# Three moves around an attention phase: late statistics of two sequences, a table preload one block earlier, bias pieces made after the plan

## The chip, the cores and the metric

The kernel runs on one core of a Trainium2 chip. A core has five engines that run side by side and meet only at semaphores: TensorE (PE in the profile, its weight loads PEld), VectorE (DVE), ScalarE (ACT), GpSimd (POOL) and SyncE (SP, which here only issues DMAs). The metric is the device time in microseconds of one launch; lower is better. All data are fp32 unless said otherwise.

## The reference, cut to what matters

Input x is 16 sequences of 512 tokens with 128 features. Two layers follow, each a mixing part and an expert part around a residual, with a LayerNorm and a per-sequence modulation ahead of each:

```python
h = layernorm(x) * (1 + ca) + sa;  x = x + ga * ssm(h)          # layer 0: gate, 16-state recurrence per feature, LayerNorm
h = layernorm(x) * (1 + cb) + sb;  x = x + gb * moe0(h)         # layer 0: 8 experts, the best one per token
h = layernorm(x) * (1 + ca) + sa;  x = x + ga * linear_attention(h)   # layer 1: 16 heads, softplus of q and k
h = layernorm(x) * (1 + cb) + sb;  x = x + gb * moe1(h)         # layer 1: 8 experts, swiglu, the best two per token
```

`layernorm` needs for each token the mean and the variance over its 128 features. Softplus is computed as relu(z) plus a corrected log(1 + exp(-|z|)). The second matrix of `moe1` has a bias b2 per expert (8 x 128 numbers), which a matmul adds.

## The kernel before, in words

The tokens stay in SBUF in one buffer `x_tok`: partition = token within a tile of 128, then 64 tiles of 128 features; a sequence is C = 4 tiles. B is 16. The program is a chain of blocks with a barrier between them (`end_phase`, L67: all engines meet, the phase's semaphores are cleared, all engines meet again). The blocks that matter:

**The mixture** (layer 0's experts, to L1143). Each engine has its instructions for sequences w = 0 to 15 in an order written out by hand. For each w, DVE masks the features by expert (`mask`), PE multiplies (`product`), ACT scales the result (`scaled`), PE turns it back and DVE adds it to `x_tok` (`added`). Behind that stand the statistics that the next LayerNorm needs: DVE sums a sequence (`sum_x2`), ACT squares it with an accumulating output, four instructions and four reads (`squares_2`), and POOL makes from both the factor `rs2` = (variance + eps)^-0.5 and the shift `shift2` = -mean * rs2 (`mean_2`, `scale_2`). So `rs2` and `shift2` of all 16 sequences are there when the block ends.

**The attention** (from L1389). All engines but SP run a written loop of bodies n; in body n each works on several sequences at once, each at another stage. DVE's body n holds `correction(n)`, `logits(n - 5)`, the softplus of n, four `weighted(n - 1, c)`, `moments(n - 2)` (bn_stats and bn_aggr of the tokens after the attention) and `added(n - 5)`. PE waits in its `states` for the softplus. ACT numbers its bodies three ahead of DVE: ACT's body n holds `exponentials(n - 3)` and also `norm0(n)`, which normalizes sequence n's tokens with `rs2` and `shift2`; it is the only reader of these two. ACT uses Ln and Exp in turn, which one table set holds; at the block's start ACT loads that set (L1721).

At the block's start SP issues small loads one after the other: keys' bias, weights, b2 (into a part of `xg`, the buffer of layer 0 that the attention doesn't use, called `room`), 8 loads of `bv`, 8 of `wo`, last the router's weights and their bias `gb`. DVE's opening instructions split two biases into bf16 pieces whose sum is the fp32 value: the keys' bias (`bkf`, L1812) and b2 (`b2f` into `b2x`, L1819 to L1828), the latter a memset, then twice a cast, a product and a subtraction, then a cast, on 3 partitions of 1024 numbers. Then DVE waits for `gb` (L1829), sets up constants and enters the loop.

POOL multiplies keys and values (`products`, L1515) and sends each token's normalized features to its two experts' rows in DRAM (`send`, L1524: 128 indirect DMAs, eight per sequence, in the kernel's text scatters).

**The plan** (from L2066). When the last sequence's experts are known, DVE works out how many tiles each expert has and where each starts, in a chain of short instructions that ends with `packs` (L2107); its widest use two scratch tensors `ge` and `gst` in `room`. SP waits for all scatters and for the plan, then loads the first rows.

**The experts of layer 1** (to the end): 72 tiles of 256 rows. PE multiplies (L2494, L2515) and adds b2 from `b2x` (L2510), from its third tile on; DVE and ACT work on both halves of the product.

## Time and profile before

| what | value |
|---|---|
| time, median of 3 runs | 981.67 us (980.34 to 982.22) |
| profiled execution | 986.01 us, span 984.10 us |
| PE busy | 839.7 us, 85% of the span |
| DVE busy | 775.3 us, 79% |
| ACT busy | 658.5 us, 67% |
| POOL busy | 562.5 us, 57% |
| chain that ended last | PE 52%, DVE 3%, DMA 3%, issue 2% |

The span runs from the first to the last instruction of the profiled execution; around it lie 1.91 us that belong to its time. An engine's busy share says little by itself, since the phases have different limits; the page's slices show the phases:

```profile
PE   6978891699999939999999999998306999999991
```
```profile
DVE  2988678899998766779999999999753666666996
```
```profile
PEclk9989795699999969999999999999557999999996
```

Each digit is a slice of 24.6 us, in tenths; PEclk is the clock granted to PE, in tenths of full speed. The mixture ends in slice 14, the attention runs to slice 28, the plan lies in slices 28 to 30, and the experts of layer 1 fill the rest.

### The profile page before, as it was taken

Reading aid. Unit: us, or ns where it says so; the run is one execution under the profiler, and the core shown is the slowest. Engines: PE = TensorE matmul, PEld = TensorE weight load, DVE = VectorE, ACT = ScalarE, POOL = GpSimd, SP = SyncE. Lnnn points to the kernel's source line nnn. Section 1 sums busy time; section 2 is a strip of 40 time slices with the busy share of each in tenths; the row PEclk is TensorE's granted clock in tenths of the full one; section 3 lists DMA queues with packets and bytes.
Section 4 is the critical chain, followed back from the end, with each engine's and each line's share of the span. In section 5 each row is a group of like instructions: output and inputs, shape, how many; then the busy total and the mean of one; then the engine's idle time right before and its main releaser. Section 6 shows DMA issues by size and latency. Waiting matters only on the chain.

```text
span 984.1 us, 23471 instructions
## 1 busy us (share of the span) xinstructions
PE 839.7 (85%) x7426; PEld 649.8 (66%) x7441; DVE 775.3 (79%) x2069; ACT 658.5 (67%) x1737; POOL 562.5 (57%) x573
## 2 busy tenths in 40 slices
PE   6978891699999939999999999998306999999991
PEld 5945570354445428888888888887105889889880
DVE  2988678899998766779999999999753666666996
ACT  3557127899995375667777787764605888888880
POOL 1211007747873325343888888888772666666773
PEclk9989795699999969999999999999557999999996
DMA  5330262233233121000111111111125655555977
GB/s 149 91 92 1 87 174 61 97 130 114 98 129 114 60 45 46 2 1 21 37 35 37 35 45 37 34 37 42 47 94 157 221 182 178 183 182 187 338 247 252
DMA packets 83813, 101.31 MB, mean 103 GB/s; under 512 B 15390, under 2 KB 65497, under 8 KB 81516
## 3 DMA queue, kind: packets, MB, share of 16 engines
q1 hardware_dynamic: 71100, 79.46, 25.5%
q0 software_dynamic: 8704, 18.11, 5.3%
q10 hardware_dynamic: 3888, 2.25, 0.7%
q8 instruction: 62, 1.02, 0.4%
q14 instruction: 59, 0.48, 0.2%
HBM read 76.11 MB, written 23.67 MB: 101 GB/s over the span
## 4 chain that ended last, share of the span: by engine, by line
PE 52%; DVE 3%; DMA 3%; issue 2%; POOL 1%; ACT 1%; SPq 1%; ACTq 0%; POOLq 0%; DVEq 0%
PE ps L2494 13%; PE ps L2251 11%; PE ps L2515 6%; PE ps L2267 3%; PE ps L2329 2%; PE ps L2242 2%; PE ps L2477 2%; PE ps L2213 2%; PE ps L2388 2%; PE ps L2368 2%; PE ps L2262 2%; PE ps L2228 1%; POOL rows_of L1524 1%; PE ps L2316 1%; DMA parts<-gx,dest 1%
## 5 line engine op out<-in xcount | busy, mean ns | idle before, releaser
L1524 POOL DMA_INDIRECT rows_of<-payb,posu x128 | 146.1, 1141 | 40.6 <-issue 27.1
L1515 POOL TENSOR_TENSOR kvb<-qk,v 128x1024 f32<-128x1024 f32 x64 | 126.1, 1975 | 75.0 <-DVE qk L1889 50.3
L1115 PE MATMUL ps<-masked,ew 128*128 128x512 f32 x256 | 130.0, 623 | 4.1 <-DVE masked L1043 3.5
L2251 PE MATMUL ps<-con,kvb 128*128 128x128 f32 x1024 | 126.0, 276 | 0.0
L2251 PEld LDWEIGHTS ps<-con,kvb 128*128 128x128 f32 x1024 | 119.4, 192 | 1.0 <-issue 1.0
L2176 DVE TENSOR_SCALAR qk<-ps,b 128x256 f32<-128x256 f32 x144 | 62.9, 478 | 69.7 <-PE ps L2494 67.1
L1549 POOL DMA_INDIRECT parts<-h,dest x72 | 71.0, 986 | 52.5 <-ACT h L1791 38.5
L1043 DVE TENSOR_TENSOR masked<-f_t,wide 128x512 f32<-128x512 f32 x128 | 88.3, 707 | 9.8 <-PE ps L1115 9.5
L1865 DVE TENSOR_TENSOR qc<-ps,qk 128x1024 f32<-128x1024 f32 x64 | 78.1, 1220 | 18.4 <-PE ps L2251 17.8
L1549 POOL DMA_INDIRECT parts<-gx,dest x72 | 73.6, 1023 | 32.6 <-issue 17.4
L2515 PE MATMUL ps<-w,f_t 128*128 x576 | 76.1, 275 | 0.0
L2515 PEld LDWEIGHTS ps<-w,f_t 128*128 128x128 f32 x576 | 70.0, 192 | 8.3
L1115 PEld LDWEIGHTS ps<-masked,ew 128*128 128x128 f32 x256 | 43.4, 194 | 46.9 <-issue 24.0
L1777 ACT ACTIVATE qk<-ps,b 128x256 f32<-128x256 f32 x144 | 60.5, 471 | 17.3 <-PE ps L2494 16.6
L2494 PE MATMUL ps<-qd,ex 128*128 128x256 f32 x288 | 69.5, 385 | 0.0
L2494 PE MATMUL ps<-qd,lg 128*128 128x256 f32 x288 | 68.2, 380 | 0.0
L2494 PEld LDWEIGHTS ps<-qd,ex 128*128 128x128 f32 x288 | 53.0, 194 | 6.0
L1782 ACT ACTIVATE nrm<-qk,limit 128x512 f32<-128x512 f32 x72 | 52.0, 723 | 7.2 <-ACT qk L1777 0.4
L891 ACT ACTIVATE junk<-x_tok,stat 128x128 f32<-128x128 f32 x128 | 49.4, 387 | 10.4 <-DVE stat L1019 9.8
L2142 DVE SCALAR_TENSOR_TENSOR f_t<-qk,nrm 128x512 f32<-128x512 f32 x72 | 49.9, 693 | 7.8 <-ACT nrm L1782 1.0
L2494 PEld LDWEIGHTS ps<-qd,lg 128*128 128x128 f32 x288 | 51.9, 190 | 5.8 <-ACT qd L1762 0.2
L1762 ACT ACTIVATE qd<-ps,ns 128x256 f32<-128x256 f32 x72 | 34.2, 474 | 30.4 <-PE ps L2477 30.4
(347 smaller groups left out, 2133.5 us busy)
## 6 DMA issues: line engine op xcount, KB each, us to landing
wide<-hot_dram SPq DMA_DIRECT2D x16, 1024.0 KB, 4.6
kvb<-rows_of SPq DMA_DIRECT2D x72, 132.0 KB, 2.5
ex<-in_w_dram SPq DMA_DIRECT2D x36, 256.0 KB, 2.8
lg<-in_w_dram SPq DMA_DIRECT2D x36, 256.0 KB, 2.8
toep<-taps_dram SPq DMA_DIRECT2D x16, 512.0 KB, 5.8
xg<-parts SPq DMA_DIRECT2D x16, 512.0 KB, 5.6
x_tok<-in_x_dram SPq DMA_DIRECT2D x16, 256.0 KB, 2.8
rows<-rows_dram SPq DMA_DIRECT2D x16, 192.0 KB, 3.1
```

The costliest lines, as they stand in the source:

```text
L1043: nc.vector.tensor_tensor(masked[e % 4][:, :], f_t[w % W][:, :], wide[w % W][:, e, :], ALU.mult).then_inc(s["masked"], 1)
L1115: nc.tensor.matmul(ps[:, w % 2, :], ew0[:, e, :], masked[e % 4][:, :], start=False, stop=(e == E - 1)).then_inc(s["product"], 1)
L1515: nc.gpsimd.tensor_tensor(kv[g % KB][:, :, :].rearrange("p e (h d) -> p e h d", h=H), k_in, v_in, ALU.mult).then_inc(s["kv"], 1)
L1524: nc.gpsimd.indirect_dma_start(rows_of, bass.IndirectOffsetOnAxis(ap=posu[w % 2][:, slot, t:t + 1], axis=0), pay[w % PB][:, t, :], None).t ...
L1549: nc.gpsimd.indirect_dma_start(parts, bass.IndirectOffsetOnAxis(ap=dest[:, u, c:c + 1], axis=0), yw[u][:, c, :], None).then_inc(s_out[u], 16)
L1777: last = nc.scalar.activation(glu[v % 2][:, f, :], ps[:, bank, f * SP:(f + 1) * SP], ACT.Relu, bias=b1[:, bass.ds(e * NF + f, 1)], scale=-1.0)
L1782: nc.scalar.activation(gs[v % 2][:, :, :], glu[v % 2][:, :, :], ACT.Gelu_apprx_sigmoid, bias=limit[:, :], scale=-1.0).then_inc(m["gs"], 1)
L1865: nc.vector.tensor_tensor(qc[g % 2][:, :, :], cum(g), q_in, ALU.mult).then_inc(s["qc"], 1)
L2176: last = nc.vector.tensor_scalar(lin[v % 2][:, f, :], ps[:, bank + 1, f * SP:(f + 1) * SP], b1[:, bass.ds(e * NF + 2 + f, 1)], 8.0, ALU.ad ...
L2251: last = nc.tensor.matmul(cum(g)[:, e, :], kv[g % KB][:, e, :], k("upto"), start=True, stop=True)
L2494: last = nc.tensor.matmul(ps[:, bank + f // 2, (f % 2) * SP:(f % 2 + 1) * SP], w1c[v % WC][:, f * P:(f + 1) * P], x_t[v % 2][:, :], start= ...
L2515: last = nc.tensor.matmul(to, act_t[v % 2][:, j, c * P:(c + 1) * P], w2[:, bass.ds(e * (2 * D) + j * D, D)], start=False, stop=(c == S - 1 ...
```

## The change

The statistics of sequences 14 and 15 leave the mixture: POOL's `mean_2`, `scale_2`, ACT's `squares_2` and DVE's `sum_x2` of both are gone. In the attention, DVE makes their mean and variance with bn_stats and bn_aggr (`late_moments`) in its bodies 5 and 7, ACT makes `rs2` with Ln and Exp (`late_root`) in its bodies 9 and 11, and DVE makes `shift2` (`late_shift`) in its bodies 8 and 10; `norm0` waits for that count. The table set for Ln and Exp is loaded as ACT's last instruction of the mixture, not as its first of the attention. The splitting of b2 stands behind the plan, not ahead of the loop, and `ge` and `gst` lie further up in `room`, so that they don't cover `b2f`. The diff, cut to its core:

```diff
@@ mixture, POOL @@
-                    mean_2(11); mean_2(12); scale_2(10); scale_2(11); scale_2(12); mean_2(13); mean_2(14); scale_2(13); scale_2(14)
-                    mean_2(15); scale_2(15)
+                    mean_2(11); mean_2(12); scale_2(10); scale_2(11); scale_2(12); mean_2(13); scale_2(13)
@@ mixture, ACT @@
-                    squares_2(14); squares_2(15)
+                    nc.scalar.preload_act_table_set("natural_log_exp_and_others")
@@ mixture, DVE @@
-                    added(14); sum_x2(14); added(15); sum_x2(15)
+                    added(14); added(15)
@@ attention, tiles @@
-            ge, gst = (room[:, q * BT * E3:(q + 1) * BT * E3].rearrange("p (b e) -> p b e", e=E3) for q in range(2))
+            ge, gst = (room[:, 2 * E * D + q * BT * E3:2 * E * D + (q + 1) * BT * E3].rearrange("p (b e) -> p b e", e=E3) for q in range(2))
+            LATE = 2
+            late_st = sb("late_st", [P, C, 6], scope=sc)
+            late_mv = sb("late_mv", [P, LATE, C, 2], scope=sc)
@@ attention, ACT @@
+                    def late_root(w):
+                        j = w - (B - LATE)
+                        need(act, "init", 3)
+                        need(act, "late_mv", j + 1)
+                        rs = rs2[:, w * C:(w + 1) * C]
+                        nc.scalar.activation(rs, late_mv[:, j, :, 1], ACT.Ln, bias=eps[:, :]).then_inc(s["late_lv"], 1)
+                        need(act, "late_lv", j + 1)
+                        nc.scalar.activation(rs, rs, ACT.Exp, scale=-0.5).then_inc(s["late_rs"], 1)
 ...
                     def norm0(w):
                         if exists(w):
                             need(act, "turned", w - 1)
+                            need(act, "late_sh", w + 1 - (B - LATE))
 ...
-                    nc.scalar.preload_act_table_set("natural_log_exp_and_others")
                     for n in range(B + 8):
 ...
                         variance_root(n - 6)
+                        if n in (9, 11):
+                            late_root(B - LATE + (n - 9) // 2)
                         logits_kept(n - 8)
@@ attention, DVE @@
-                    nc.vector.memset(b2x[:, :], 0.0)
-                    dve.wait_ge(m["bias"], 16)
-                    for j in range(2):
-                        nc.vector.tensor_copy(b2h[:, :], b2f[:, :]).then_inc(m["split"], 1)
-                        dve.wait_ge(m["split"], 3 * j + 1)
-                        nc.vector.tensor_scalar(b2r[:, :], b2h[:, :], which[:, j:j + 1], None, ALU.mult).then_inc(m["split"], 1)
-                        dve.wait_ge(m["split"], 3 * j + 2)
-                        nc.vector.tensor_tensor(b2f[:, :], b2f[:, :], b2r[:, :], ALU.subtract).then_inc(m["split"], 1)
-                        dve.wait_ge(m["split"], 3 * j + 3)
-                    nc.vector.tensor_copy(b2x[0:3, :], b2f[:, :]).then_inc(m["split"], 1)
                     dve.wait_ge(s["weights"], 3 * 16)
 ...
+                    def late_moments(w):
+                        j = w - (B - LATE)
+                        need(dve, "late_mv", j)
+                        for c in range(C):
+                            last = nc.vector.bn_stats(late_st[:, c, :], tile(w, c))
+                        last.then_inc(s["late_st"], 1)
+                        need(dve, "late_st", j + 1)
+                        for c in range(C):
+                            last = nc.vector.bn_aggr(late_mv[:, j, c, :], late_st[:, c, :])
+                        last.then_inc(s["late_mv"], 1)
+
+                    def late_shift(w):
+                        j = w - (B - LATE)
+                        need(dve, "late_rs", j + 1)
+                        at = slice(w * C, (w + 1) * C)
+                        nc.vector.scalar_tensor_tensor(shift2[:, at], late_mv[:, j, :, 0], -1.0, rs2[:, at], ALU.mult, ALU.mult).then_inc(s["late_sh"], 1)
 ...
                         if n == 4:
                             numbers()
+                        if n in (5, 7):
+                            late_moments(B - LATE + (n - 5) // 2)
+                        if n in (8, 10):
+                            late_shift(B - LATE + (n - 8) // 2)
                         added(n - 5)
@@ behind the plan, DVE @@
                     dve.wait_ge(s["plan"], n[0])
+                    (the ten lines taken out above, unchanged)
                     need(dve, "red", B * C)
```

## Rows read from the trace of the kernel before

**Rows 1.** Stretches: start:end, length, busy (instructions) per engine, PE's clock, DMA share, GB/s.
```profile
core 0: us, PE busy (x) PEld busy (x) DVE busy (x) ACT busy (x) POOL busy (x), PEclk, DMA share, GB/s
345.00:351.00 6.00, 0.00 (x0) 0.00 (x0) 1.32 (x2) 2.33 (x12) 3.02 (x7) 0.77 0.00 0
364.00:376.00 12.00, 8.16 (x55) 7.25 (x57) 9.45 (x16) 7.16 (x12) 6.02 (x4) 0.72 0.58 132
376.00:684.00 308.00, 304.13 (x3300) 260.36 (x3307) 274.86 (x698) 215.71 (x544) 223.69 (x149) 1.00 0.09 29
```

**Rows 2.** Timeline at the ends of two phases (start, length, engine, line; idle before).
```profile
147.77 0.60 ACT L627 ACTIVATE xg<-ps 128x512 f32<-128x512 f32 x1 [1.19 <-PE ps L702]
...
149.78 0.34 SPq L783 DMA_DIRECT2D rows<-rows_dram  x1
...
343.46 0.69 ACT L932 ACTIVATE moe_t<-ps,mod_t 128x512 f32<-128x512 f32 x1 [2.62 <-PE ps L1115]
...
344.95 0.69 DVE L1014 TENSOR_TENSOR x_tok<-x_tok,ps 128x512 f32<-128x512 f32 x1 [3.28 <-PE ps L1103]
...
349.51 0.20 POOL L832 TENSOR_TENSOR shift<-shift,rs 128x4 f32<-128x4 f32 x1
...
351.11 0.27 SPq L1392 DMA_DIRECT2D bkf<-in_bqkv_dram  x1
...
351.12 1.28 ACT L1721 ACT_TABLE_LOAD   x1 [3.08 <-PEq L70]
```

**Rows 3.** Timeline of DVE, first microseconds of the attention.
```profile
356.49 0.48 DVE L1819 MEMSET b2x<- 128x512 uint32 x1
...
356.90 0.62 DVE L1822 CAST b2h<-xg 3x1024 bf16<-3x1024 f32 x1
...
357.56 0.74 DVE L1824 TENSOR_SCALAR xg<-b2h,which 3x1024 f32<-3x1024 bf16 x1
...
358.33 1.22 DVE L1826 TENSOR_TENSOR xg<-xg 3x1024 f32<-3x1024 f32 x1
...
363.48 0.24 DVE L1830 TENSOR_SCALAR gw<-gw,ns 128x32 f32<-128x32 f32 x1 [0.48 <-DMA gb<-in_gb_dram]
```

**Rows 4.** Timeline of DVE, bodies 5 to 8 of the attention.
```profile
465.31 0.86 DVE L1922 BATCH_NORM_STATS2 st<-x_tok 128x6 f32<-128x128 f32 x4
...
466.51 0.66 DVE L1895 TENSOR_TENSOR qd<-ps,qk 128x512 f32<-128x512 f32 x1
...
467.09 1.26 DVE L1954 TENSOR_TENSOR x_tok<-x_tok,gx 128x512 f32<-128x512 f32 x1
...
474.25 1.22 DVE L1865 TENSOR_TENSOR qc<-ps,qk 128x1024 f32<-128x1024 f32 x1 [0.32 <-PE ps L2251]
...
475.77 0.19 DVE L1960 TENSOR_TENSOR logit<-ps,gb 128x32 f32<-128x32 f32 x1 [0.30 <-PE ps L2436]
...
515.13 1.23 DVE L1865 TENSOR_TENSOR qc<-ps,qk 128x1024 f32<-128x1024 f32 x1 [0.50 <-PE ps L2251]
```

**Rows 5.** Timeline of POOL and ACT in the same stretch.
```profile
465.81 1.98 POOL L1515 TENSOR_TENSOR kvb<-qk,v 128x1024 f32<-128x1024 f32 x1
...
474.64 0.28 ACT L1713 ACTIVATE lg_t<-ps 128x128 f32<-128x128 f32 x1 [0.81 <-PE ps L2424]
```

**Rows 6.** Timeline of DVE and POOL, from the plan to the first expert tile.
```profile
724.26 1.96 DVE L2096 TENSOR_TENSOR xg<-number,first 128x1728 f32<-128x1728 f32 x1
...
725.10 1.95 POOL L1524 DMA_INDIRECT rows_of<-payb,posu  x1 [0.30 <-issue]
...
731.73 0.17 DVE L2107 CAST packs<-packf 128x9 int32<-128x9 f32 x1
...
739.44 0.96 POOL L1524 DMA_INDIRECT rows_of<-payb,posu  x1 [0.30 <-issue]
...
751.70 0.48 DVE L2176 TENSOR_SCALAR qk<-ps,b 128x256 f32<-128x256 f32 x1 [19.79 <-PE ps L2494]
```

**Rows 7.** Timeline of DVE in the mixture, a cast.
```profile
169.00 1.25 DVE L1031 CAST ebh<-ebf 24x128 bf16<-24x128 f32 x1
```

**Rows 8.** Timeline of PE, its states of the first sequence.
```profile
368.19 1.78 PE L2388 MATMUL ps<-v,qk 128*128 128x144 f32 x6 [3.43 <-DVE qk L1889]
```

More of the change, by code:

```diff
@@ L1264, in build @@
                      "pay", "pay_ps", "pay_t", "gx", "x4", "lg_ps", "lg_t", "lg_back", "lg", "max", "idx", "idf", "hot", "ed", "ee", "e1", "p1", "taken", "counted", "carried",
-                     "rank_ps", "rank", "sel", "pos", "posu", "extra", "labels", "totals", "base", "place", "pads", "experts", "plan", "padrow", "beside")
+                     "rank_ps", "rank", "sel", "pos", "posu", "extra", "labels", "totals", "base", "place", "pads", "experts", "plan", "padrow", "beside", "late_st", "late_mv", "late_lv", "late_rs", "late_sh")
             s = {nm: sem(f"p3_{nm}") for nm in names}
@@ L2108, in _ @@
                     dve.wait_ge(s["plan"], n[0])
+                    nc.vector.memset(b2x[:, :], 0.0)
+                    dve.wait_ge(m["bias"], 16)
+                    for j in range(2):
+                        nc.vector.tensor_copy(b2h[:, :], b2f[:, :]).then_inc(m["split"], 1)
+                        dve.wait_ge(m["split"], 3 * j + 1)
+                        nc.vector.tensor_scalar(b2r[:, :], b2h[:, :], which[:, j:j + 1], None, ALU.mult).then_inc(m["split"], 1)
+                        dve.wait_ge(m["split"], 3 * j + 2)
+                        nc.vector.tensor_tensor(b2f[:, :], b2f[:, :], b2r[:, :], ALU.subtract).then_inc(m["split"], 1)
+                        dve.wait_ge(m["split"], 3 * j + 3)
+                    nc.vector.tensor_copy(b2x[0:3, :], b2f[:, :]).then_inc(m["split"], 1)
                     need(dve, "red", B * C)
```

## The prediction

> **What bounds the kernel now.** I read the table of stretches first, then the timeline around each place that the diff touches, then the chain of waits. In the attention (376 to 684) PE is busy 304.13 of 308.00 us at a granted clock of 1.00 [rows 1]: there the time is PE's own, and another engine matters only where it makes PE wait. Between the phases PE has nothing (345 to 351: zero matmuls, [rows 1]); there the time is that of whichever engine ends the mixture last, plus the barrier. From the last scatter to the first expert tile the chain of waits runs over POOL's scatters, a DMA and SP. So three places decide: the end of the mixture, the two or four attention bodies that get new work, and the stretch behind the plan.
>
> **1. The mixture's end.** PE's last matmuls release DVE's `added(15)`, which runs 344.95 to 345.64. Behind it stand `sum_x2(15)`, eight squares with their reads on ACT, and POOL's `scale_2(15)`, whose last instruction ends at 349.71. SP's first instruction of the attention starts at 351.11, 1.40 us later [rows 2]. The diff takes those statistics out for sequences 14 and 15. What ends last is then one of three. DVE: 345.64. ACT: its `scaled(15)` starts at 343.46 and lasts 0.69, so ends at 344.15; behind it now comes the table load, 1.28 us in the row at 351.12, so 345.43. POOL: `scale_2(13)` waited for squares long made, and ends before either. DVE is last at 345.64, which is 4.07 us before 349.71.
> The price of the barrier could depend on who comes last. At the end of the phase before, ACT was last (147.77 + 0.60 = 148.37) and SP started at 149.78: 1.41 us, against 1.40 with POOL last [rows 2]. I take the same for DVE. **Term: -4.07.** Bounds: -4.3 (some engine starts its barrier part early) to -3.8.
>
> A rule that speaks against this is in the Trainium skill, "ScalarE: Activation LUTs", section "What ACT_TABLE_LOAD costs": a switch is 1283 ns of load and about 1380 ns of drain, some 2.66 us. By that rule ACT would end at 344.15 + 2.66 = 346.81 and be last, and the term would be -2.90. The row has only the 1.28.
>
> **2. The attention's first body.** DVE made b2's pieces here, from the memset at 356.49 to 363.00; then it waited 0.48 us for the DMA of `gb` and went on at 363.48 [rows 3]. Taking 6.5 us of work away from in front of a wait that ends at 363.48 gives nothing: the wait is for SP's queue, which issues 23 DMAs one after the other, that of `gb` the last (the b2 load is still among them). The table load at 351.12 [rows 2] delayed ACT by 1.28 at the start, but what ACT makes is used by DVE's correction only after the same wait. **Term: 0**, bounds 0 and -0.48 (if the landing were not the limit). What is late next is the same `gb`.
>
> **3. New work in the attention.** DVE gets, in its bodies 5 and 7, four bn_stats and four bn_aggr. The same eight for `moments` start at 465.31 and the next instruction at 466.51: 1.20 us [rows 4]. Against it stand DVE's idle times in the next body, in front of the second `weighted` (0.32 behind body 5, 0.50 behind body 7) and in front of `logits` (0.30; the one behind body 7 is alike) [rows 4]. PE waits for the softplus that comes after these, and it comes just in time for PE, so what exceeds the idle time is lost once: 1.20 - 0.62 = 0.58 and 1.20 - 0.80 = 0.40, together 0.98 at most. But the new instructions read one tensor, and they are put just ahead of `added(n-5)`, which took 1.26 us at 467.09 because POOL's product of 465.81 to 467.79 ran [rows 4, 5]: 0.70 of it lies under POOL. The new work fills that time, and `added` then finds the way free: 1.20 - 0.70 = 0.50, under the 0.62 of idle. In body 7 I expect half of that relief, so about 0.85 against 0.80. The two `late_shift` (bodies 8 and 10) are one instruction of four columns each, in bodies with 0.8 us idle. ACT's two extra pairs of Ln and Exp (about 0.5 us a pair) come right in front of `logits_kept`, where ACT waits 0.81 us for PE [rows 5]; their inputs are made before ACT gets there. `norm0(14)` waits for a value made four bodies earlier. **Term: +0.1**, bounds 0 and +1.0; I take the value by the relief, since the blocked `added` is in the row itself.
>
> **4. b2's pieces behind the plan.** DVE is idle for 19.79 us before its first expert tile at 751.70 [rows 6], so 6.5 us from 731.8 to 738.3 are hidden on DVE. PE needs the pieces at its third tile, later still. But beside it POOL issues its last seven scatters, each 0.96 us and 0.30 apart, the last at 739.44; a scatter's landing, SP's wait and the first tile hang on them. And the trace shows that DVE can hold them up: the scatter at 725.10 took 1.95 us instead of 0.96, while DVE ran a tensor_tensor of two SBUF operands from 724.26 to 726.22 [rows 6]; it ended 0.83 us after that one did. So a scatter asks for something about 0.13 us after its start, waits for the DVE instruction that runs then, and needs 0.83 more. Do casts hold it too? In the other direction the cast at 169.00 took 1.25 us for 128 columns, where one of 1024 takes 0.62 [rows 3, 7]; POOL was in its additions to x_tok then. So a cast shares whatever it is.
> Laid out: the memset starts at 731.83 behind the row at 731.73 and the rest keeps the spacing of [rows 3]: cast 732.24 to 732.86, tensor_scalar to 733.64, subtraction to 734.89, cast to 735.6, tensor_scalar to 736.4, subtraction to 737.6, cast to 738.3. The scatters started at 731.87 and then every 1.26 us. The second (733.13, asks at 733.27) waits for 733.64 and ends at 734.47, 0.37 late. The third asks at 734.90, in the gap behind a subtraction. The fourth asks at 736.16, waits for 736.38, and is 0.59 late in all; the fifth asks at 737.64, again in a gap; the last two are free. **Term: +0.6.** If only the two subtractions held scatters it would be 0.55. Two of these gaps are hit by 0.02 us: missing the later one makes it 1.3, missing both 1.8. Bounds: 0 and +1.8, unless scatters can't slip in between two DVE instructions (below).
>
> The Trainium skill, "SBUF — State Buffer", in its box on the "DVE blocks DMA" trap, says that while DVE runs a two-port mode instruction GpSimd is locked out and can't write the descriptors of its DMAs. This trace agrees for the two-operand instruction (1.95 against 0.96); for casts in front of scatters no row of it shows the effect. [...]
>
> **Sum.** -4.07 + 0 + 0.1 + 0.6 = -3.4 us. The profiled execution took 986.01 us with a span of 984.10; the sum makes that 982.6. It was 4.3 us over the median of the runs shown (981.67), so the forecast for the median is 981.67 - 3.4 = 978.3, its own range 977.3 to 979.6.
>
> **Rivals.**
> A. The covers are thinner than counted: DVE's new work costs PE the 0.98, and the scatters miss both gaps (1.8). For it: PE takes the softplus the moment it is made, and the gaps are 0.03 us wide. Against: the blocked `added`. Sum -4.07 + 1.0 + 1.8 = -1.3: 980.4, not to be told from no change.
> B. PE's clock. PE stops at 344.92 and the clock is at its higher level (2.4 GHz) until about 348.2, then at half: 0.77 over the six microseconds [rows 1]. With the phase starting 4.07 earlier, and ACT's first norms 1.28 earlier still, PE gets its first work that much sooner, perhaps before the clock falls. In 364 to 376 the clock is 0.72 on the mean, 6.7 us at half; PE waits 3.43 us there and then starts its states at 368.19 [rows 1, 8], on the chain. If the clock came back before this, up to 3.9 us of matmuls would take half: -1.9, sum -5.3: 976.4. Against: that wait stays, and it is after it that the clock is low.
> C. Slower. DVE holds the shared way over its whole run of pieces, because its gaps of 0.03 us admit no scatter. The second scatter would then wait from 733.27 to 738.34 and end at 739.17; five more follow at 1.26, the last starting at 744.5 instead of 739.44: +5.1. Sum +1.1: 982.8; with the first scatter caught by the memset +6.3, sum +2.4: 984.1. It decides against the kernel once the scatters lose more than 4.0 us. Against: the scatter of 725.10 ended at 727.05, in the midst of the next DVE instruction of that length, so it got in between.
> D. The change doesn't do what it says for the table: preloaded in one block it is not known in the next, and loads are put between Ln and Exp. At 1.28 us, two in each of 16 bodies, that is up to +41: 1019. Against: the mixture's block shows no table load of its own, though ACT's functions are used in it.
> E. The table load keeps ACT from the barrier for longer than its row. At twice the 1.28 us ACT would end at 344.15 + 2.56 = 346.71, last by 1.07, and the sum is -3.0 + 0.7 = -2.3: 979.4. Against: the row at 351.12 is 1.28 long and no more. (The drain of the page named under 1 would make it 979.5.)
>
> **How the numbers follow.** Forecast 0.60, A 0.18, B 0.10, C 0.05, D 0.02, E 0.05. The range 976.0 to 981.0 takes in the forecast, A, E and most of B; C and D and small parts of the others are outside. About 0.2% (2 us) is what a measurement here can tell from no change. Over 2 us faster: nearly all of the forecast, B, half of E: 0.70. Within: A and the rest: 0.24. Slower: 0.06.
>
> **What would show it.** SP's first issue of the attention at about 347.0, with a table load ahead of it and none behind; `gb` landing 12.4 us after it, as before. Bodies 6 and 8 no longer than their neighbours by over 0.2 us, `added` of body 5 at 0.66 us instead of 1.26. Some of the last seven scatters over 0.96 us, the last at 739.44 - 4.0 + 0.6 = about 736.0. Wrong would be: a phase start later than 347.5 (terms 1, E), PE stalls in bodies 6 and 8 (term 3), scatters late by over 1.5 us (term 4), or PE's states at the clock's higher level (B).

## The result, and the profile after

Over 15 runs the changed kernel takes 984.97 us (982.66 to 986.93), the kernel before beside it 982.30. The ratio is 1.0023, with an interval of 1.0012 to 1.0033: slower by about 2.3 us, where 3.4 us less was forecast. The forecast was wrong in its sign, and 984.97 lies outside its range.

The profiled execution of the changed kernel took 983.36 us, with a span of 981.6. That is 2.5 us less than the 984.1 before, the other way than the medians. The stages tell why. Their marks are instructions that both kernels have: SP's first `rows` load of the mixture, its first load of the attention, the first and the last of DVE's 16 reciprocals `rden` (one to a sequence), SP's first `kvb` row load of the experts.

| stage, us | before | after | difference |
|---|---|---|---|
| start of the span to the mixture | 149.78 | 144.25 | -5.53 |
| the mixture | 201.33 | 196.99 | -4.34 |
| attention, to the first `rden` | 25.77 | 25.99 | +0.22 |
| first to last `rden` | 298.51 | 304.86 | +6.35 |
| last `rden` to the experts | 68.07 | 69.25 | +1.18 |
| the experts | 240.64 | 240.26 | -0.38 |

The first row is code that the diff doesn't touch. It took 144.1 to 149.8 us in the profiled executions of the 14 kernels of this study, and I leave it out. The other five sum to +3.03, which agrees with the +2.7 of the medians. So every comparison below goes by stages. From one execution to another the mixture varies by some 0.7 us, the last two rows by 1.2 and 1.4, and a loop without new work in its full bodies by 0.2 or less.

The mixture's end, answering to [rows 2], is as predicted:

```profile
337.69 0.69 ACT L931 ACTIVATE moe_t<-ps,mod_t 128x512 f32<-128x512 f32 x1 [2.62 <-PE ps L1114]
338.40 1.28 ACT L955 ACT_TABLE_LOAD   x1
...
339.19 0.69 DVE L1013 TENSOR_TENSOR x_tok<-x_tok,ps 128x512 f32<-128x512 f32 x1 [4.00 <-PE ps L1102]
...
341.24 0.27 SPq L1394 DMA_DIRECT2D bkf<-in_bqkv_dram  x1
```

DVE is last, at 339.88, and SP starts 1.36 us later. The table load ends at 339.68, under DVE's addition. The attention's start, answering to [rows 1, 3, 8], is as before too: DVE now waits 7.05 us for the same `gb`, and PE's clock (0.72) and its wait before its states (3.42 us) are what they were.

```profile
353.63 0.24 DVE L1833 TENSOR_SCALAR gw<-gw,ns 128x32 f32<-128x32 f32 x1 [7.05 <-DMA gb<-in_gb_dram]
...
358.34 1.78 PE L2422 MATMUL ps<-v,qk 128*128 128x144 f32 x6 [3.42 <-DVE qk L1892]
```

The stretches of the changed kernel (columns as in [rows 1]; the first is that of 364 to 376 before, shifted by the 9.87 us by which the attention starts sooner):

```profile
354.13:366.13 12.00, 8.14 (x48) 7.08 (x51) 9.25 (x16) 6.13 (x11) 5.81 (x3) 0.72 0.58 135
...
376.00:684.00 308.00, 299.25 (x3237) 255.20 (x3250) 276.94 (x718) 213.66 (x547) 221.21 (x150) 0.99 0.10 29
516.00:517.00 1.00, 0.68 (x3) 0.71 (x4) 1.00 (x3) 0.43 (x3) 0.74 (x1) 0.63 0.00 0
517.00:519.00 2.00, 2.00 (x12) 1.91 (x12) 1.74 (x4) 0.00 (x0) 1.84 (x2) 0.50 0.00 0
```

In 376 to 684 PE is busy 299.25 us where it had 304.13. It now waits for DVE's softplus; the waits of that stretch on PE, after and then before (waited for, total, times, longest):

```profile
PE ps L2422 <- DVE qk L1892: 5.1, 5, 2.1
```
```profile
PE ps L2388 <- DVE qk L1889: 0.7, 3, 0.4
```

The intervals of the loop, from one `rden` to the next and counted from 0, around the new work:

```
interval     4      5      6      7      8      9
before   20.42  20.36  20.35  20.34  20.35  20.34
after    23.06  19.62  23.53  22.62  19.31  20.35
```

Interval 4 contains the statistics of body 5, interval 6 those of body 7, interval 7 what follows in body 8. The first pair costs 1.9 us, the following three intervals 4.4. Here is what lengthened interval 4, on DVE and POOL of the changed kernel, answering to [rows 4, 5]:

```profile
457.43 0.86 DVE L1938 BATCH_NORM_STATS2 late_st<-x_tok 128x6 f32<-128x128 f32 x4
458.32 0.38 DVE L1942 BATCH_NORM_AGGREGATE late_mv<-late_st 128x2 f32<-128x6 f32 x4
458.62 0.66 DVE L1974 TENSOR_TENSOR x_tok<-x_tok,gx 128x512 f32<-128x512 f32 x1
...
459.76 0.68 DVE L1961 TENSOR_TENSOR h<-h,rows 128x512 f32<-128x512 f32 x1
460.48 2.77 DVE L1963 TENSOR_TENSOR h<-h,rows 128x512 f32<-128x512 f32 x1
```
```profile
456.15 1.98 POOL L1517 TENSOR_TENSOR kvb<-qk,v 128x1024 f32<-128x1024 f32 x1
458.30 1.01 POOL L1526 DMA_INDIRECT rows_of<-payb,posu  x1 [0.17 <-issue]
459.62 1.05 POOL L1526 DMA_INDIRECT rows_of<-payb,posu  x1 [0.31 <-issue]
460.70 1.98 POOL L1517 TENSOR_TENSOR kvb<-qk,v 128x1024 f32<-128x1024 f32 x1
```

The new work takes the 1.2 us that it should, and `added` (L1974) takes 0.66 instead of 1.26, as the prediction said. But something else grew. Each body works on `h` with two instructions, a multiplication (L1961) and behind it an addition (L1963). The addition takes 2.77 us here, where it took 0.72 before, and POOL's next product of keys and values started 0.22 us after it. The addition, the product, and the scatter that POOL issues ahead of them, in the kernel before:

```profile
469.54 0.72 DVE L1943 TENSOR_TENSOR h<-h,rows 128x512 f32<-128x512 f32 x1
```
```profile
467.95 1.27 POOL L1524 DMA_INDIRECT rows_of<-payb,posu  x1 [0.17 <-issue]
...
470.51 1.98 POOL L1515 TENSOR_TENSOR kvb<-qk,v 128x1024 f32<-128x1024 f32 x1
```

There the product came 0.97 us after the start of an addition of 0.72 us. Counted from the product before it (465.81, and 456.15 after), the addition starts at 3.73 before and 4.33 after, so DVE is 0.60 late (1.20 less the 0.60 that `added` gives back). The next product starts at 4.70 before and 4.55 after, so POOL is 0.15 early, since its first scatter took 1.01 instead of 1.27. These 0.75 us turned 0.97 into 0.22. That scatter is what matters: before, it started 0.86 us behind the start of `added` (467.95 against 467.09) and ended 0.87 us behind its end; after, it starts 0.32 us ahead of `added` (458.30 against 458.62) and is not held. In the end the addition ends 0.57 us after the product does, 463.25 against 462.68. PE then stands for its softplus:

```profile
473.46 0.97 PE L2422 MATMUL ps<-v,qk 128*128 128x144 f32 x6 [2.09 <-DVE qk L1892]
...
516.32 1.78 PE L2422 MATMUL ps<-v,qk 128*128 128x144 f32 x6 [1.78 <-DVE qk L1892]
```

In body 7 the multiplication is the one that is caught, with 3.14 us instead of 0.68 (502.54, product at 503.13), and in body 8, where no statistics are, it takes 2.65 us (product at 525.74). After the wait of 1.78 us the granted clock is 0.50 for 517 to 519, the lower level, and the six matmuls of 516.32 take 1.78 us instead of 0.97.

Body 8 goes with that clock. PE comes later to what ACT waits for (`p_t`, the rows turned round for the router): ACT starts on it 4.98 us behind 516.32, and 3.37 us behind 473.46, where the clock stays at 1.00. ACT then normalizes `h` later, and DVE waits for it in front of the multiplication, a wait that bodies 5 to 14 of the kernel before don't have:

```profile
525.64 2.65 DVE L1961 TENSOR_TENSOR h<-h,rows 128x512 f32<-128x512 f32 x1 [0.54 <-ACT h L1718]
```

Last, the scatters behind the plan, answering to [rows 6], on POOL and on DVE:

```profile
726.52 0.95 POOL L1526 DMA_INDIRECT rows_of<-payb,posu  x1 [0.30 <-issue]
727.78 1.99 POOL L1526 DMA_INDIRECT rows_of<-payb,posu  x1 [0.30 <-DMA rows_of<-payb,posu]
730.07 1.66 POOL L1526 DMA_INDIRECT rows_of<-payb,posu  x1 [0.30 <-issue]
732.04 1.19 POOL L1526 DMA_INDIRECT rows_of<-payb,posu  x1 [0.30 <-issue]
```
```profile
727.85 0.48 DVE L2133 MEMSET b2x<- 128x512 uint32 x1
728.25 0.62 DVE L2136 CAST b2h<-xg 3x1024 bf16<-3x1024 f32 x1
728.90 0.74 DVE L2138 TENSOR_SCALAR xg<-b2h,which 3x1024 f32<-3x1024 bf16 x1
729.68 1.21 DVE L2140 TENSOR_TENSOR xg<-xg 3x1024 f32<-3x1024 f32 x1
730.93 0.68 DVE L2136 CAST b2h<-xg 3x1024 bf16<-3x1024 f32 x1
731.64 0.74 DVE L2138 TENSOR_SCALAR xg<-b2h,which 3x1024 f32<-3x1024 bf16 x1
```

Three scatters end at 729.77, 731.73 and 733.23. Less 0.83 us these are 728.94, 730.90 and 732.40, and at 728.87, 730.89 and 732.38 the first cast, the subtraction and the second tensor_scalar end. Over 0.96 us they take 1.03, 0.70 and 0.23: 1.96 us. Counted from `packs`, the plan's last instruction, the last scatter starts 9.68 us later instead of 7.71. That the stage grew by 1.18 only is because the run of scatters began 0.8 us sooner after the last `rden` (the twelfth from the end at +47.65 instead of +48.45).

### The profile page after: what moved, and what is told of

It is laid out like the page before. It is cut to its first block and busy times, and to the rows that moved or that the text cites. A ratio compares the mean times of both kernels' runs of the same rounds, so it can differ in the third digit from the quotient of the medians.

```text
span 981.6 us, 23463 instructions
## 1 busy us (share of the span) xinstructions
PE 834.9 (85%) x7426; PEld 646.5 (66%) x7441; DVE 780.6 (80%) x2085; ACT 656.2 (67%) x1725; POOL 561.5 (57%) x565
## 5 line engine op out<-in xcount | busy, mean ns | idle before, releaser
L2285 PE MATMUL ps<-con,kvb 128*128 128x128 f32 x1024 | 126.8, 277 | 0.0
L2511 PE MATMUL ps<-con,kvb 128*128 128x128 f32 x144 | 28.1, 277 | 29.9 <-DMA kvb<-rows_of 29.9
```

Source lines behind the costliest of these rows:

```text
L2285: last = nc.tensor.matmul(cum(g)[:, e, :], kv[g % KB][:, e, :], k("upto"), start=True, stop=True)
```

## The experiments

**One part at a time, and one place changed.** Four kernels, beside the kernel before at 982.06. The first has the statistics alone (table load and b2's pieces where they were), the second b2's pieces alone, the third the table load alone. The fourth is the changed kernel with the statistics moved within the body:

```diff
 (e4, against the changed kernel)
-                        if n in (5, 7):
-                            late_moments(B - LATE + (n - 5) // 2)
                         added(n - 5)
                         prefixes(n)
                         modulated(n - 3)
+                        if n in (5, 7):
+                            late_moments(B - LATE + (n - 5) // 2)
```

> Only the statistics move; table load and b2's pieces stay where they were before. Theory T (in bodies 5 and 7 the 1.2 us of new work lets POOL's product of 1.98 us start ahead of DVE's multiply or add on h, which then waits for it, 2.1 to 2.7 us each time, and the slip reaches body 8): mixture 4.1 us shorter, attention 6 to 6.5 us longer, in all 2 us slower than before, some 984.3. Rival W (what is lost is b2's work behind the plan and the later table; the attention's own loss belongs to one execution): 3 to 4 us faster than before, about 979.

Measured: 983.09 us, ratio 1.0023 (1.0007 to 1.0039). Mixture 196.92, loop 305.89, last `rden` to the experts 69.11. So the statistics alone carry both the gain and the loss: -4.41 and +7.38. The pattern is not quite that of the changed kernel. The intervals are 23.08, 22.72, 22.76 and 20.41 from number 4 on: here body 6, not body 8, is the one that is caught without statistics in it. PE waits as long as in the changed kernel (2.08 us at 473.61, there 2.09 at 473.46), but this time the clock falls behind the wait. The stretch of 476 to 477 of this kernel, the same of the changed kernel, and DVE's multiplication in body 6 of this kernel:

```profile
476.00:477.00 1.00, 1.00 (x7) 1.00 (x6) 1.00 (x7) 0.00 (x0) 0.68 (x1) 0.50 0.00 0
```
```profile
476.00:477.00 1.00, 1.00 (x12) 1.00 (x11) 1.00 (x7) 0.17 (x1) 0.54 (x1) 1.00 0.00 0
```
```profile
482.96 2.43 DVE L1971 TENSOR_TENSOR h<-h,rows 128x512 f32<-128x512 f32 x1 [1.04 <-ACT h L1717]
```

This sorts all eight waits of PE for the softplus of over 1.5 us in the loops of this study. Behind five of them PE's clock went to 0.50 (this one; 1.78 us in the changed kernel; 1.68 in e4; 1.74 and 1.81 in e9), and in each of the five the next body has an instruction caught too (in e9 once in a body with statistics of its own). Behind three it stayed at 1.00 (2.09 in the changed kernel and in e12, 2.01 in e4), and the next body is clean.

> Only b2's pieces move behind the plan. T: the last scatters are held up, three of seven by 0.2 to 1.0 us each, last scatter 1 to 2 us later than in the kernel before, the start of the attention unchanged: 1 to 2 us slower. Rival (the scatters' delay is caught by a wait further on, or the start of the attention gains from the work taken away): within 0.3 us of before.

Measured: 986.0 us, ratio 1.0038 (1.0020 to 1.0056). Loop 298.42, last `rden` to the experts 68.86, and the same three held scatters: 2.00, 1.66 and 1.18 us. The start of the attention, expected unchanged, took 26.68, 0.91 more than before: 21 to 24 us after SP's first load PE's clock is 0.66 there, and 1.00 in the kernel before. From the last `rden` to the experts it is 0.79 more. The two are 1.7 of the 3.7 us; the rest I can't place.

> Only the table load moves to the mixture's end, behind all squares. T: ACT ends its squares at 348.0 and the load at 349.3, under POOL's last scale at 349.7, and in the attention's first microseconds SP's loads set the end: no difference (within 0.3 us). Rival (the load is on the way to the first softplus): 1.3 us faster. Rival (load plus a drain of its own holds the barrier): 1 us slower.

Measured: 981.7 us, ratio 1.0001 (0.9988 to 1.0014); mixture 201.59, attention to the first `rden` 25.84, loop 298.55. Alone, the table load is worth nothing either way.

> The changed kernel with the late moments of bodies 5 and 7 put behind the multiply and add on h, everything else alike: the same instructions in the same bodies. T: multiply and add keep their place against POOL's product and no DVE instruction on h is over 1 us long; what is left is 1.2 us against DVE's idle time of 0.6 to 0.8 in the next body, at most 1.0 us for both bodies; 5 us faster than the changed kernel, some 980. Rival V (the amount of work is what costs, in whatever place): as the changed kernel, 985. Rival S (ACT's late roots or DVE's late shift in body 8 do it): as the changed kernel too, with body 8 long.

Measured: 984.12 us, ratio 1.0034 (1.0021 to 1.0047); loop 304.15, intervals 21.59, 20.99, 21.36, 24.16, 19.31 from number 4 on. The theory in the form that blamed the place in the body fell here. Multiplication and addition on `h` of bodies 5 and 7 are spared, and another instruction is caught behind each, DVE's correction, which takes 1.15 us otherwise (DVE and POOL of this kernel):

```profile
464.42 2.83 DVE L1879 SCALAR_TENSOR_TENSOR ex<-lg,ex 128x1024 f32<-128x1024 f32 x1
```
```profile
464.17 1.99 POOL L1517 TENSOR_TENSOR kvb<-qk,v 128x1024 f32<-128x1024 f32 x1
```

What stayed of it, called T from here on: a delay of DVE against POOL, wherever it arises, puts some DVE instruction with two SBUF operands into a product of 1.98 us.

**The same work elsewhere in the loop.** All against the changed kernel:

```diff
 (e6 and e5)
-                        if n in (5, 7):
-                            late_moments(B - LATE + (n - 5) // 2)
+                        if n in (1, 2):
+                            late_moments(B - LATE + n - 1)
 (e6 only: the eight instructions of b2's pieces go back to the attention's start)
 (e8: late_tile is one bn_stats and one bn_aggr; late_shift in 8 and 11, late_root in 10 and 14)
+                        if 3 <= n < 11:
+                            late_tile(n - 3)
 (e9: late_shift in 8 and 10, late_root in 10 and 12)
+                        if 5 <= n < 9:
+                            late_tile(2 * (n - 5))
+                            late_tile(2 * (n - 5) + 1)
```

> The changed kernel with two edits: the statistics of the last two sequences made in attention bodies 1 and 2 instead of 5 and 7, and b2's pieces made at the start of the attention again, as before. The stretch of the 16 denominators took 298.51 us before, 304.86 changed. Theory T (what costs is the order of DVE against POOL's key-value products: a DVE delay of tenths of a us, in a body in which PE already follows DVE closely, makes a two-operand DVE instruction wait out a product of 1.98 us, and PE loses about 2 us, in this body and the next two): bodies 1 and 2 have 3.2 us of idle DVE and no product is in the way of a late one, so the stretch is 298.5 to 299.0, the tail as before (68.1), the mixture 4.3 shorter: in all 4.0 to 4.4 us less than before, median 0.9955 of it (977.5 to 978.5). Rival V (the added work costs wherever it stands, 6.3 us for two times 1.2 us of DVE's time): stretch 304 to 305, median 1.002. Rival S (ACT's late roots or DVE's late shifts in bodies 8 to 11 cost, not the moments): these stand where they stood, so the stretch is again about 304.5.

Measured: 978.71 us, ratio 0.9968 (0.9956 to 0.9980), so 3.1 us faster, under the 4.0 to 4.4 expected. Loop 298.41, mixture 197.54. The tail is what was missed: 69.10 instead of the 68.1 of before. It is 69.11 in e1, the other kernel with late statistics and the pieces where they were.

> The changed kernel with only the statistics moved to bodies 1 and 2; b2's pieces stay behind the plan. T: the stretch of the 16 denominators as in e6 (298.5 to 299.0); behind it the last scatters are held by b2's pieces, as in the changed kernel, so from the last denominator to the first row of the mixture of experts 1.0 to 1.2 us more than in e6, and the median 0.5 to 1.5 us above e6 (978.5 to 979.5). V and S: stretch 304 to 305, median like the changed kernel's 985.

Measured: 980.08 us, ratio 0.9975 (0.9957 to 0.9992). Loop 298.52, last `rden` to the experts 70.02 against e6's 69.10. That stage alone varies as much: it is 68.86 to 70.02 in the kernels that make the pieces behind the plan. From `packs` to the last scatter is the firmer measure: 9.67 to 9.70 us in all of these, 7.71 in the kernel before, 8.99 in e1 and e6. ACT's roots stand where they stood in the changed kernel, so they cost nothing (S falls); and the work itself costs nothing in these bodies.

> The changed kernel with the same statistics spread out: one tile of 128 rows (one bn_stats, one bn_aggr, some 0.35 us with its wait) in each of bodies 3 to 10, instead of four in body 5 and four in body 7. T: a delay of 0.35 us is under the idle time that DVE has in each body (0.8 us), but whether it flips an order against POOL depends on the phase: no body over 20.6 us and the stretch 298.5 to 299.5 if it doesn't, one or two bodies of 22 to 23 if it does (each with a DVE instruction of over 2.2 us beside a product), stretch 300.5 to 303. V (PE loses in proportion to the work wherever it stands): bodies 3 to 10 each 0.4 to 0.8 us longer, none by 2, stretch 303 to 305.

Measured: 979.13 us, ratio 0.9973 (0.9960 to 0.9986). Loop 298.45, no interval over 20.42 where the work stands. All the work is there, most of it in bodies as full as those of the changed kernel, and the loop is 0.06 us shorter than in the kernel before. V would have it at 303 to 305.

> As e8, but two tiles (some 0.65 us) in each of bodies 5 to 8. T: 0.65 us is what moved body 5's h-addition in front of the product in the changed kernel, so at least one body of 22 to 23.5 us, with a DVE two-operand instruction of over 2.2 us in it, the others 20.35 or less; stretch 300.5 to 305. V: bodies 5 to 8 each 1.5 us longer, none by over 2. No flip at all (stretch under 299.5) would say that the bound lies between 0.65 and 1.2 us.

Measured, in one execution: 987.87 us; loop 306.68, intervals 20.63, 22.78, 23.04, 21.82, 22.72, 19.32 from number 4 on. The work is the same, laid over four bodies, and the loss is 8.2 us. The first of the following rows is again the addition on `h`, the second POOL's product 0.21 us behind it:

```profile
483.05 2.76 DVE L1959 TENSOR_TENSOR h<-h,rows 128x512 f32<-128x512 f32 x1
```
```profile
483.26 1.99 POOL L1517 TENSOR_TENSOR kvb<-qk,v 128x1024 f32<-128x1024 f32 x1
```

My expectation had body 5 flip (the order turn round) at 0.65 us; the two tiles took 0.82 and it didn't. What sorts the cases is POOL's first scatter behind the product. In the kernel before it starts 0.86 us behind the start of `added` in body 5 and 0.53 in bodies 6 and 7, and the new work stands in front of `added`, so it moves `added` towards the scatter. Both in body 5 of e9, then both in body 6:

```profile
460.46 0.66 DVE L1970 TENSOR_TENSOR x_tok<-x_tok,gx 128x512 f32<-128x512 f32 x1
460.52 1.48 POOL L1526 DMA_INDIRECT rows_of<-payb,posu  x1 [0.17 <-issue]
...
480.92 1.01 POOL L1526 DMA_INDIRECT rows_of<-payb,posu  x1 [0.17 <-issue]
...
481.19 0.66 DVE L1970 TENSOR_TENSOR x_tok<-x_tok,gx 128x512 f32<-128x512 f32 x1
```

In microseconds, from the start of `added` to that of the scatter:

| kernel, body | new work | before, less the new work | measured | the scatter took | caught |
|---|---|---|---|---|---|
| before, 5 | 0 | 0.86 | 0.86 | 1.27 | none |
| e8, 5 | 0.41 | 0.45 | 0.46 | 1.27 | none |
| e8, 6 | 0.41 | 0.12 | 0.12 | 1.42 | none |
| e9, 5 | 0.82 | 0.04 | 0.06 | 1.48 | none |
| e9, 6 | 0.81 | -0.28 | -0.27 | 1.01 | the addition, 2.76 |
| changed, 5 | 1.20 | -0.34 | -0.32 | 1.01 | the addition, 2.77 |
| changed, 7 | 1.20 | -0.67 | -0.64 | 1.01 | the multiplication, 3.14 |

A scatter that starts behind `added` is held and ends 0.87 to 0.90 us behind its end, and so POOL waits as long as DVE is late: the next product still comes 0.95 to 0.98 us after the start of the addition, whatever the new work. A scatter that starts ahead of `added` runs through DVE's bn_stats and bn_aggr in 1.01 us, POOL goes on, and the product meets DVE. In bodies 5 to 14 of the twelve kernels with the whole product there are 120 such scatters: 108 of them are held, and neither multiplication nor addition on `h` is caught behind any; 12 are free (three in the changed kernel, three in e1, one in e4, four in e9, one in e12), and one DVE instruction is caught behind each, in body 7 of e1 and of e9 the running sum of the states (3.09 and 3.10 us where 0.64 is usual). The corrections caught in e4 are another meeting, later in the body. No run moves that scatter alone, so its part is read from these traces and not tested by itself.

**One body alone, a thin product, and the scatters.** The first is the changed kernel with this; the next two (one execution each) are the kernel before and the changed one with POOL's product cut to one of its eight value columns; e7 is e5 with a wait.

```diff
 (e12)
-                        if n in (5, 7):
-                            late_moments(B - LATE + (n - 5) // 2)
+                        if n in (1, 5):
+                            late_moments(B - LATE + (n - 1) // 4)
 (e10 and e11)
-  v_in = v1[w % 2][:, c, 0:HD, :].unsqueeze(3).to_broadcast([P, HD, H, HD])
-  nc.gpsimd.tensor_tensor(kv[g % KB][:, :, :]...
+  v_in = v1[w % 2][:, c, 0:1, :].unsqueeze(3).to_broadcast([P, 1, H, HD])
+  nc.gpsimd.tensor_tensor(kv[g % KB][:, 0:1, :]...
 (e7, in front of b2's memset behind the plan)
+                    for j in range(PB):
+                        dve.wait_ge(s_scat[j], 16 * SCATTERS * (B // PB))
```

> The changed kernel with the statistics of sequence 14 in body 1 and those of sequence 15 in body 5, so that only body 5 has new work where it hurt. In the changed kernel bodies 5 and 6 together took 1.9 us over their neighbours and bodies 7 to 9 4.4 us. T: body 5 about 23.0 and body 6 about 19.6 us, the others 20.35: stretch 300.3 to 300.6 against 298.5 before, and the median 980 to 982.5. If one flip leaves the bodies behind it exposed and they flip too, the stretch is 302.5 or more. V: half of 6.3, stretch 301.5 to 301.9, spread over the body and not in one instruction.

Measured: 981.11 us, ratio 0.9993 (0.9976 to 1.0010). Loop 300.49, intervals 23.06, 19.63, 20.35, 20.35: one flip costs 1.98 us and heals by itself, with PE's clock at 1.00 behind the wait. The rows of that body and PE's wait behind it repeat those of the changed kernel:

```profile
461.58 2.76 DVE L1963 TENSOR_TENSOR h<-h,rows 128x512 f32<-128x512 f32 x1
```
```profile
474.57 0.97 PE L2422 MATMUL ps<-v,qk 128*128 128x144 f32 x6 [2.09 <-DVE qk L1892]
```

> The kernel before, with POOL's key-value product computing one of its eight columns of values (the other seven are zero, so seven eighths of this product are left out, and the routing of the rows behind it differs). The stretch of the 16 denominators is to be compared with e11 alone; as PE sets 20.35 us a body, both theories expect 297 to 299 us here, and POOL's product at 0.3 to 0.5 us instead of 1.98.

> The changed kernel with the same thin product. T (the loss is a DVE instruction that waits out a product of 1.98 us): with a product under 0.5 us there is nothing long to wait for, so the stretch is within 1.0 us of e10's, and no two-operand DVE instruction of bodies 5 to 8 takes over 1.6 us. V (the loss is the time that the statistics take on DVE): the stretch is 5 to 7 us over e10's, as 304.86 against 298.51. A result between (2 to 4 us over) would say that both take part.

Measured: loop 297.40 before and 297.41 after. With the thin product the whole difference of 6.35 us is gone, though the statistics stand in bodies 5 and 7: intervals 21.27, 19.26, 21.20, 19.30, each pair 40.5 us as in e10. No DVE instruction of bodies 5 to 8 is caught. Nor is it that a thin product leaves DVE more room: from interval 4 on its idle time per interval is 0.80 us in e10 and 0.62 to 0.80 in the kernel before. So the wait for the product is the cause. The addition on `h` of body 5 met a product 0.23 us after its start here as well, but a short one, and it took its usual time; e11's DVE and POOL:

```profile
459.09 0.86 DVE L1939 BATCH_NORM_STATS2 late_st<-x_tok 128x6 f32<-128x128 f32 x4
...
461.69 0.69 DVE L1962 TENSOR_TENSOR h<-h,rows 128x512 f32<-128x512 f32 x1
462.42 0.69 DVE L1964 TENSOR_TENSOR h<-h,rows 128x512 f32<-128x512 f32 x1
```
```profile
462.65 0.72 POOL L1518 TENSOR_TENSOR kvb<-qk,v 128x128 f32<-128x128 f32 x1 [0.21 <-PE ps L2286]
```

Its product took 0.72 us there and 0.41 in bodies 3 and 4, so when both are short it is the product that gives way, or both share. What decides who goes first I can't tell.

> As e5 (statistics in bodies 1 and 2, b2's pieces behind the plan), but the pieces wait until all scatters have landed. In e5 three scatters took 2.00, 1.66 and 1.18 us beside these pieces, 1.96 us in all over the usual 0.96. If the pieces are what holds them, all scatters behind the plan take 0.95 to 0.96, the last one comes 1.9 to 2.1 us sooner behind the start of the plan, DVE still ends the pieces before its first expert tile, and the median is 1 to 2 us below e5's 980.1. If the pieces' holding costs nothing because something else ends there last, the median stays within 0.5 us of 980.1.

Measured: 977.65 us, ratio 0.9946 (0.9927 to 0.9964). All scatters behind the plan take 0.95 to 0.96 us, the last one at +64.11 after the last `rden` instead of +66.00 (-1.89), and the experts start at +68.13 instead of +70.02. The pieces end in time, at 740.55; DVE still waits 3.47 us for PE behind them:

```profile
734.05 0.48 DVE L2135 MEMSET b2x<- 128x512 uint32 x1 [10.10 <-DMA rows_of<-payb,posu]
...
744.02 0.88 DVE L2212 TENSOR_SCALAR qk<-ps,b 128x256 f32<-128x256 f32 x2 [3.47 <-PE ps L2530]
```

This is the fastest version of the study, 4.8 us under the kernel before by the medians. e5 was timed beside other executions of the kernel before (981.85, here 982.44) and the two intervals just overlap, so the lead over e5 rests on the stage as well. Between e7 and e6 the runs don't decide.

## Why the prediction was wrong

- **Term 1, the mixture's end: -4.07, right.** DVE was last, as said; 341.24 - 339.88 = 1.36 to SP's first load instead of 1.40. From DVE's last addition to that load it is 5.47 us before and 1.36 after, so -4.11; the stage has -4.34, the further 0.23 lying earlier in the mixture. With the table load under the addition, E did not show: SP's load follows DVE's end by the usual 1.4. Nor did the drain that the Trainium skill, "ScalarE: Activation LUTs", section "What ACT_TABLE_LOAD costs", adds to a load: by its figure ACT would have ended at about 341.06 (an estimate: 339.68 + 1.38), 0.18 us before SP's start, where the three barriers measured here took 1.36 to 1.41; and in the kernel before, the instruction behind ACT's load of 751.13 starts at 752.42, 0.01 us after the 1.28 are over. D fell too: no second load stands in the attention.
- **Term 2, the first body: 0, right** (+0.22). B's clock stayed at 0.72 over the same twelve microseconds, with PE waiting 3.42 us in front of its states, as was held against B.
- **Term 3, the statistics in bodies 5 and 7: +0.1 forecast, +6.35 measured. This step failed.** Its parts held in the main: 1.20 us of new work, 0.60 of relief in `added` (the sum used 0.70), the idle times on DVE. The step set the rest against DVE's idle time, with every other duration taken as it was. It left out that these durations depend on where POOL stands. The rows had the price and I read only its good half: `added` at 467.09 took 1.26 beside the product of 465.81 to 467.79 [rows 4, 5], so it ended 0.56 after the product, and in the changed kernel all three caught instructions end 0.56 to 0.57 after theirs. I counted one instruction that leaves such a meeting, and didn't ask which enters one. The question had an answer in the trace: POOL's first scatter starts 0.86 us behind `added` in body 5 and 0.53 in body 7, and 1.20 us of work ahead of `added` is more than either. With DVE's delay alone the product would have come 0.97 - 0.60 = 0.37 after the addition, and this would have taken 0.37 + 1.98 + 0.56 = 2.91 instead of 0.72, some 2.2 us late (measured: 0.22 and 2.77, so 2.05); e12 measured 1.98 for one such body. Two of them at 2.2 are +4.4, and the sum becomes -3.4 - 0.1 + 4.4 = +0.9, on the other side. The rest of the 6.35 is body 8, which flips in the wake of body 7, and PE's drop to the lower clock, with which it goes. In e12, e4 and the changed kernel the clock stays up behind the body that comes first, and its neighbour is clean; in e1 it falls, and the neighbour flips. Why it fell there after 2.08 us and not in the others after 2.09 and 2.01 stays open.
- **Term 4, b2's pieces: +0.6 forecast, 1.96 measured in the scatters, mis-sized.** The mechanism held to 0.07 us: a scatter ends 0.83 us after the DVE instruction that it waits for. Cast, tensor_scalar and subtraction all held scatters. The box on the "DVE blocks DMA" trap in the Trainium skill, "SBUF — State Buffer", speaks of two-port mode instructions alone; the prediction called its row of a two-operand instruction an agreement, which the box doesn't cover. Here the measurement decides: the scatter beside the subtraction, which has two SBUF operands, lost 0.70 us. The term failed by its first line, which let the scatter at the memset go free; it was held until the cast behind the memset ended, 1.03 us. Gaps of 0.03 to 0.04 us did let scatters in, against C. What it costs the kernel shows in e7 against e5: with the scatters free, the last one and the experts both come 1.89 us sooner.
- **The rivals.** A had the right place and a sixth of the price, as it stopped at 0.98 us of DVE's own time. No rival had the order between DVE and POOL.
- **The range** held neither result nor sign, because every bound of term 3 was a sum of DVE's own times. A bound by the nearest bad row, one caught instruction in each of the two bodies at 2.2 us, would have put the upper end at 978.3 + 4.3 = 982.6 at the least.

## What to carry to other kernels

Where two engines keep each other out of SBUF, work added to one of them is not paid in its own time. It shifts an order, and the price is the length of the other engine's instruction. Before putting work into a tight loop, look for the place where the other engine waits for yours and is kept in step by it (here a scatter that starts 0.86 or 0.53 us behind `added`), and ask whether the new work lets it slip past. Work short enough to leave that order alone is free (e8: eight pieces of 0.41 us) where larger pieces of the same work cost 8 us (e9, one execution); and a body with real slack takes all of it at once (e5, e6). Where TensorE stalls, look at its clock behind the stall: whether the next body was caught too went with it in all eight cases here.

## What the runs showed of the hardware that I had not expected

- A DVE instruction with two SBUF operands that meets POOL's product of 1.98 us waits nearly all of it: 0.7 us becomes 2.43 to 3.14, 1.15 becomes 2.83, also where DVE had started 0.22 or 0.59 us ahead. DVE instructions that read PSUM beside the same product keep their time: `qc` took 1.21 at 463.76 in the changed kernel, with the product at 464.15.
- A memset and a cast in succession hold a scatter as well, for 1.03 us here, and it then takes the time it needs from the end of that cast, 0.83 us.
- bn_stats and bn_aggr don't hold a scatter: it took 1.01 us beside them in the changed kernel (458.30), where `added` holds one that starts behind it until 0.87 us past its own end.
- One wait of 1.78 us in a loop where PE is otherwise full was followed by over two microseconds at the lower clock (1.2 GHz). After the wait of 2.09 us at 473.46 the same matmuls took 0.97, the time at the higher one. After the wait of 2.08 us at 473.61 in e1 the clock was at 1.00 until 475 and at 0.50 to 0.51 from there to 478.
